# One block for attention and experts in a decoder layer on one core: first shared weights fetched and rounded inside attention, slots computed before other work

## What is computed

```python
x = layernorm(x + state_space_and_mlp(x))           # selective scan, 8 heads, and an MLP of 1024
x = layernorm(x + cross_and_self_attention(x, ctx)) # 16 heads of 128, 4 key/value heads
x = layernorm(x + experts(x))

# experts, on 1024 tokens of 256 channels
scores = sigmoid(x @ w_router.T)                    # 8 experts
topk_w, topk_i = top_k(scores, 2); topk_w /= topk_w.sum(-1)
out = sum over the 2 chosen e: topk_w * ((silu(x @ wg[e].T) * (x @ wu[e].T)) @ wd[e].T)   # inner width 640
out += sum over 2 shared experts j: (silu(x @ sg[j].T) * (x @ su[j].T)) @ sd[j].T
```

## Time and profile before

| what | us |
|---|---|
| median of 3 runs (lowest, highest) | 779.17 (778.35, 784.29) |
| profiled execution | 787.61 |
| its span, first to last instruction | 785.9 |
| PE busy | 722.3 (92%) |
| DVE busy | 564.8 (72%) |
| ACT busy | 472.9 (60%) |
| POOL busy | 344.0 (44%) |

### The profile page before, as it was taken

One profiled execution on the slowest core, in us unless ns is written; L12 is line 12 of the kernel. 1 busy time (PEld: TensorE's weight loads), 2 busy tenths in 40 slices (PEclk: granted clock), 3 DMA queues, 4 the chain that ended last, 5 costly groups with the idle time before them and its releaser, 6 DMA issues. The chain is left out here.

```text
span 785.9 us, 15318 instructions
## 1 busy us (share of the span) xinstructions
PE 722.3 (92%) x5030; PEld 657.3 (84%) x5030; DVE 564.8 (72%) x1176; ACT 472.9 (60%) x1066; POOL 344.0 (44%) x512
## 2 busy tenths in 40 slices
PE   4998888788999999999999987998999999999965
PEld 3887677577889999999899976986999999999855
DVE  4864588876878888887878773664587778776436
ACT  4454666456877777777777772342577777776301
POOL 0002566596988787877787751063000000000341
PEclk9999999998999999999999999699999999999978
DMA  9003300100200000000600000266356766670121
GB/s 290 4 1 115 134 2 0 30 5 28 62 8 1 7 0 7 0 7 0 207 0 0 0 1 9 96 240 209 115 161 227 250 203 210 227 241 28 54 67 54
DMA packets 45940, 64.82 MB, mean 82 GB/s; under 512 B 4288, under 2 KB 34880, under 8 KB 45632
## 3 DMA queue, kind: packets, MB, share of 16 engines
q1 hardware_dynamic: 39936, 56.39, 21.7%
q0 software_dynamic: 1536, 4.20, 1.6%
q10 hardware_dynamic: 4416, 3.58, 1.6%
HBM read 53.14 MB, written 11.01 MB: 82 GB/s over the span
## 5 line engine op out<-in xcount | busy, mean ns | idle before, releaser
L1816 POOL DMA_INDIRECT gu_raw<-rows_out,slot x16 | 15.5, 972 | 203.6 <-DMA rows_out<-y_sb 199.0
L1951 ACT ACTIVATE sg<-bg 128x256 f32<-128x256 f32 (+1 forms) x95 | 40.7, 429 | 104.1 <-PE bg L68 101.6
L413 ACT ACTIVATE under_dt<-two,nb,under_raw 128x256 f32<-128x256 f32 x128 | 70.6, 561 | 45.5 <-DVE nb L496 45.5
L66 PE MATMUL bg<-xb_hi,gu_hi 128*128 128x256 f32 x300 | 87.0, 290 | 2.7 <-DVE xb_lo L2064 2.7
L2041 DVE TENSOR_TENSOR hf<-sg,bg 128x256 f32<-128x256 f32 (+1 forms) x95 | 45.1, 475 | 58.1 <-ACT sg L1951 56.6
L68 PE MATMUL bg<-xb_hi,gu_lo 128*128 128x256 f32 x300 | 85.6, 285 | 0.0
L67 PE MATMUL bg<-xb_lo,gu_hi 128*128 128x256 f32 x300 | 85.5, 285 | 0.0
L66 PE MATMUL two<-under_h 128*128 128x256 f32 (+1 forms) x208 | 66.9, 322 | 2.9 <-PEq L117 1.5
L68 PE MATMUL bd<-dn_hi,eh_lo 128*128 128x256 f32 x220 | 63.1, 287 | 3.9 <-issue 3.8
L67 PE MATMUL bd<-dn_lo,eh_hi 128*128 128x256 f32 x220 | 62.9, 286 | 3.0 <-issue 3.0
L594 POOL TENSOR_SCALAR under_dt<-under_dt,rec 128x256 f32<-128x256 f32 x128 | 61.5, 499 | 6.4 <-DVE rec L542 6.4
(11 more groups left out here) (294 smaller groups left out, 2555.6 us busy)
## 6 DMA issues: line engine op xcount, KB each, us to landing
gu_raw<-in_gu SPq DMA_DIRECT2D x17, 1280.0 KB
dn_raw<-in_dn SPq DMA_DIRECT2D x17, 640.0 KB
rows_in<-under_dt SPq DMA_DIRECT2D x1, 3840.0 KB, 13.1
rows_out<-y_sb SPq DMA_DIRECT2D x30, 128.0 KB, 2.1
x_blk<-rows_in ACTq DMA_DIRECT2D x13, 256.0 KB, 2.7
under_raw<-in_wq SPq DMA_DIRECT2D x1, 2048.0 KB, 8.1
under_raw<-in_wkv SPq DMA_DIRECT2D x1, 2048.0 KB, 12.7
under_raw<-in_wo SPq DMA_DIRECT2D x4, 512.0 KB, 3.9
```

What stands on the lines that cost most here:

```text
L66: pe.matmul(out, lh, rh, start=first, stop=False)
L413: act.activation(self.prob[:, g % 2, h, :], self.b_s[:, h // 2, (h % 2) * MW:(h % 2 + 1) * MW], ACT.Exp, bias=self.nb[:, h:h + 1], scale=s ...
L1816: pool.indirect_dma_start(got[k][:, b, :], None, ys[:, :], bass.IndirectOffsetOnAxis(ap=slot[:, k, b:b + 1], axis=0)).then_inc(f_got[b], 16)
L1951: act.activation(sg[:, u % 3, 0:width(u)], gate_of(u), ACT.Silu).then_inc(f_sg, 1)
```

## The change

Allocation: the experts' buffers are laid out first, over the same memory that attention uses, and released at once, so that both lie over each other; the set of buffers with index 0 and the x buffers are put on the other side. All semaphores of attention and experts are taken in the outermost scope and cleared once at the end. `experts` now returns its engine programs, and each engine's program of attention calls its program of the experts directly, in the same block. What the end of the block ensured is now waited for one by one: PE's transposes wait for the batches they read and for the last readers of the banks that they write; SP and POOL wait for all of `x_tok`.

Order: SP requests the first shared weights after attention's last projection. ACT rounds them in `act_tail`, POOL takes the remainders in `pool_tail` (before: DVE). DVE splits the first quarter of x between the statistics and the rows of batch 7, the last quarter between its first two gates. PE interleaves transposes and logits. `places` comes directly after the gate of unit 1 and before the two splits, `gated(2)` moves up behind it, `rest_dn(0)` and `shares` move to the end of pass 0. All spare products at the seam and in pass 0 go (28, 16 and 28). The load of `upper` moves from ACT's queue to SP's.

The diff, with changes of indentation left out and cut to its core:

```diff
@@ decoder_layer
+        ex = experts(nc, a, scope, sem, ident, x_tok, acc, wr, rank, s_router, xs, ys, s_zero, out)
         with ExitStack() as both:
-            at = Attention(scope(both), nc, a, ident, x_tok, s_zero, xs)
-            state_space_layer(nc, a, scope, ident, x_tok, acc, s_const, at, wr, rank, s_router)
-        experts(nc, a, scope, ident, x_tok, acc, wr, rank, s_router, xs, ys, s_zero, out)
+            at = Attention(scope(both)[0:2] + (sem,), nc, a, ident, x_tok, s_zero, xs, ex)
+            state_space_layer(nc, a, scope, sem, ident, x_tok, acc, s_const, at, wr, rank, s_router)
@@ act_tail
         self.act_p(act, N1)
+        self.ex.act_weights(act, 0)
+        self.ex.act_weights(act, 1)
         self.act_exp(act, 3, N3)
@@ dve_tails
         self.dve_tail(dve, LAST)
+        self.ex.dve_x(dve, 0)
         self.dve_tail2(dve, LAST)
@@ pool_tail
             self.pool_step(pool, LAST, g, False, True)
+            if g >= 2:
+                self.ex.pool_weights(pool, g - 2)
@@ Attention.sp_program
+        sp.wait_ge(self.a_pj, NS)
+        self.ex.load_first(sp)
@@ Attention.pe_program
         self.over_batches(pe, self.pe_step, self.pe_tail)
-        self.pe_spare(pe, self.b_q[:, 0:DM], 28)
@@ state_space_layer (and the same for sp, pool, act, dve)
                     aw.pe_program(pe)
+                    aw.ex.pe_program(pe, aw)
@@ experts
+        def load_first(sp):
+            sp.dma_start(gu_raw[0][:, :, :, :], a["gu"][E].rearrange("s (k p) n -> p s k n", p=P)).then_inc(e_gu[0], 16)
+            sp.dma_start(dn_raw[0][:, :, :], a["dn"][E].rearrange("(i p) n -> p i n", p=P)).then_inc(e_dn[0], 16)
+        def act_weights(act, s):
+            if s == 0:
+                act.wait_ge(e_gu[0], 16)
+            act.activation(gu_hi[0][:, s, :, :], gu_raw[0][:, s, :, :], ACT.Copy).then_inc(w_gh[0], 1)
+        def pool_weights(pool, s):
+            pool.wait_ge(w_gh[0], s + 1)
+            pool.tensor_tensor(gu_lo[0][:, s, :, :], gu_raw[0][:, s, :, :], gu_hi[0][:, s, :, :].bitcast(F32),
+                               ALU.subtract).then_inc(w_gl[0], 1)
+        def dve_x(dve, q):
+            s = slice(q * 256, (q + 1) * 256)
+            dve.wait_ge(r_f, q + 1)
+            dve.tensor_copy(x_hi[:, :, s], x_f[:, :, s]).then_inc(r_hi, 1)
+            dve.wait_ge(r_hi, q + 1)
+            dve.tensor_tensor(x_lo[:, :, s], x_f[:, :, s], x_hi[:, :, s].bitcast(F32), ALU.subtract).then_inc(r_lo, 1)
@@ experts, sp
-                load(0)
+            sp.wait_ge(at.a_x2, BATCH)
+            sp.wait_ge(s_zero, 16)
+            sp.dma_start(upper[:, :], a["upper"]).then_inc(r_c2, 16)
             load(1)
@@ experts, pool
+            pool.wait_ge(at.a_x2, BATCH)
+            pool.wait_ge(s_zero, 16)
@@ experts, pe
-                for q in range(4):
+            def turn_x(q):
+                pe.wait_ge(at.a_x2, 2 * q + 2)
+                if q == 0:
+                    pe.wait_ge(at.a_exp, NS * AREP)
+                elif q == 2:
+                    pe.wait_ge(at.a_olo, NS)
...
-                pe.wait_ge(r_lo, 1)
-                spare(pe, bx[1][:, 0:256], x_hi[:, 0, 0:P], x_hi[:, 0, 0:256], 16)
+            turn_x(0)
+            turn_x(1)
+            turn_x(2)
+            pe.wait_ge(s_router, 32)
+            for b in range(4):
+                logits(b)
+            turn_x(3)
+            for b in range(4, BATCH):
+                logits(b)
             for q in range(NG_):
...
-                    if q == 0:
-                        spare(pe, bd[1][:, 0:256], x_hi[:, 0, 0:P], x_hi[:, 0, 0:256], 28)
@@ experts, act
-                act.dma_start(upper[:, :], a["upper"]).then_inc(r_c2, 16)
...
-                round_gu(0, 0)
-                round_gu(0, 1)
@@ experts, dve
-                rest_gu(0, 0)
-                rest_gu(0, 1)
+            dve_x(dve, 1)
+            dve_x(dve, 2)
             dve.wait_ge(r_l, 1)
+            dve.wait_ge(s_zero, 16)
...
+                if q == 0:
+                    dve_x(dve, 3)
                 gated(IT * q + 1)
+                if q == 0:
+                    places()
+                    gated(2)
                 rest_h(IT * q)
...
                 if q == 0:
-                        places()
                     owners()
-                        rest_dn(0)
-                        shares()
...
+                if q:
                     gated(IT * q + 2)
...
                 rest_h(IT * q + 3)
+                if q == 0:
+                    rest_dn(0)
+                    shares()
```

More of the change, by code:

```diff
@@ L7 @@
+from collections import namedtuple
 from contextlib import ExitStack
@@ L158, with __init__ @@
 class Attention:
-    def __init__(self, ctx, nc, a, eye, x_tok, s_zero, xs):
+    def __init__(self, ctx, nc, a, eye, x_tok, s_zero, xs, ex):
         self.sb, self.ps, self.sem = ctx
-        self.nc, self.a, self.eye, self.x_tok, self.s_zero, self.xs = nc, a, eye, x_tok, s_zero, xs
+        self.nc, self.a, self.eye, self.x_tok, self.s_zero, self.xs, self.ex = nc, a, eye, x_tok, s_zero, xs, ex
         self.turn = {}
@@ L731, in pool_program, with state_space_layer @@
         pool.tensor_tensor(r1[:, :], ve[:, :], mh[:, 0:1], ALU.pow).then_inc(self.a_r1, 1)
-def state_space_layer(nc, a, scope, ident, x_tok, acc, s_const, aw, wr, rank, s_router):
+def state_space_layer(nc, a, scope, kept, ident, x_tok, acc, s_const, aw, wr, rank, s_router):
     with ExitStack() as layer:
-        sb, ps, sem = scope(layer)
         h_hi, h_lo, win_hi, win_lo = aw.h_hi, aw.h_lo, aw.win_hi, aw.win_lo
@@ L1146, in state_space_layer @@
         with ExitStack() as part:
-            sb, ps, sem = scope(part)
+            sem = kept
             TW = 2 * P
@@ L1221, in _ @@
                     aw.sp_program(sp)
+                    aw.ex.sp_program(sp, aw)
                 @block.gpsimd
@@ L1645, in outputs_before, with experts @@
     return sum(4 if shared(g) else 2 for g in range(q))
-def experts(nc, a, scope, ident, x_tok, accm, wr, rank, s_router, xs, ys, s_zero, out):
+Programs = namedtuple("Programs", ("load_first", "act_weights", "pool_weights", "dve_x", "sp_program", "pool_program",
+                                   "pe_program", "act_program", "dve_program"))
+def experts(nc, a, scope, sem, ident, x_tok, accm, wr, rank, s_router, xs, ys, s_zero, out):
     NG_ = NBLK + 4
@@ L1651, in experts @@
     ROOTS = ((0, 4), (4, 6), (6, 8))
[L1652 to L1660, removed]
+    with ExitStack() as over:
+        sb, ps, _ = scope(over)
+        side = lambda i: "right" if i == 0 else None
+        gu_raw = [sb(f"gu_raw{i}", [P, 2, KT, FI], F32, side(i)) for i in range(2)]
+        dn_raw = [sb(f"dn_raw{i}", [P, IT, DM], F32, side(i)) for i in range(2)]
+        gu_hi = [sb(f"gu_hi{i}", [P, 2, KT, FI], F32R, side(i)) for i in range(2)]
+        gu_lo = [sb(f"gu_lo{i}", [P, 2, KT, FI], F32R, side(i)) for i in range(2)]
+        x_hi = sb("x_hi", [P, KT, TOK], F32R, "right")
+        x_lo = sb("x_lo", [P, KT, TOK], F32R, "right")
+        x_f = sb("x_f", [P, KT, TOK], F32, "right")
         dn_hi = [sb(f"dn_hi{i}", [P, IT, DM], F32R) for i in range(2)]
```

897 lines of the change are left out of this document (444 added, 453 removed).

## The result

| | median of runs, us (lowest to highest) | profiled, us | span, us |
|---|---|---|---|
| before, the 3 runs known at first | 779.17 (778.35 to 784.29) | 787.61 | 785.9 |
| before, with the 6 taken beside the change | 783.28 (778.35 to 786.56) | | |
| the change, 9 runs | 772.57 (770.26 to 779.31) | 770.26 | 768.6 |

The ratio is 0.9874, 95% interval 0.9846 to 0.9902: some 9.9 us faster (7.7 to 12.1). The forecast was 765.7 with a saving of 13.5; 772.57 lies above its range. The sign was right, the time was not.

What follows compares the result with a forecast made beforehand. PE's spare products, waits and half clock at the seam between attention and experts were taken as the loss. A gain of 16.5 us less 3.0 for the clock, 13.5 off 779.17, gave 765.7 us; range 761.5 to 770.

Steps and rivals of the forecast that it cites:

- POOL's remainders, taken at nothing: Attention's tail: POOL takes the first shared weights' remainders, 3.0 us each, inside its idle time, at no cost.
- the base of 779.17: Median of the runs shown, 8.4 us under the profiled one; the forecast took its saving off this.
- Transposes and router: Seam: transposes directly follow attention's last product, router records take 0.12 us each, PE through at 489.4 instead of 498.07.
- Weights on ACT: Attention's tail: ACT rounds the first shared weights, 2.43 us, inside a 2.65 us wait, at no cost.
- A stretched tail: Sign that the prediction is wrong: attention's tail itself stretches, with exponentials after 469.
- First quarter of x: End of attention: DVE makes it while waiting for POOL's root; last x_tok slips by 0.1 us, at no cost.
- Places, fifth unit: First shared pass: slots at 500.0, 14.6 us earlier; the fifth unit starts at 500.8 instead of 518.22.
- Scatter late next by 0.9: First routed block: its rows arrive at 528.5, PE at 527.6, so PE waits 0.9 us; gain there 16.5 us.
- The clock: Seam: PE's clock falls during transposes and 8-column router records, costing 3.0 us, bounds 0 and 4.1.
- clock stays up: Rival, chance 0.24: the clock does not fall at the seam, saving 16.5 us, time 762.7.
- The seam as a whole: From attention's end to the first routed block: 16.5 us gained less 3.0 for the clock, 13.5 us off.
- The rival of a slower time: Chance 0.03: the clock does not come back, both shared passes run at half clock, time 793 us.

Runs made afterwards that it cites:

- e7: e1 with DVE's rounding of the first quarter of x moved behind the last normalised tokens; 769.47 us, ratio 0.9824 to the kernel before.
- e1: The change with both POOL remainders of the first shared weights moved behind its last attention step; on three chips 772.83, 768.42, 772.16 us (ratios 0.9871, 0.9797, 0.9850).
- e2: The change with two groups of 8 spare PE products added among the seam's transposes and router products; 773.08 us, ratio 0.9846 to the kernel before.
- e6: The change with each POOL subtraction of 128x1280 cut into ten of 128x128 in the same place; 770.93 us, ratio 0.9826 to the kernel before.
- e3: The change with DVE's order in pass 0 put back as in the kernel before; 779.14 us, ratio 0.9943 to the kernel before.

## Why the prediction failed, step by step

Two terms put the measured 772.57 above the range: POOL's remainders, taken at nothing, cost attention's tail 1.7 us, and the base of 779.17 was 4.1 us low. With the later base the forecast would have been 769.8, with the tail's 1.7 us as well 771.5.

- **Transposes and router: right.** They follow attention's last product directly. The record that no row had priced takes 1.92 / 16 = 0.12 us at full clock, the value taken. The 0.60 us of ACT's copy was read from a silu of the same shape; the copies took 0.60 too.
- **Weights on ACT: right**, inside its idle time. **Remainders on POOL, "nothing": wrong.** The step looked at idle time on POOL's own queue and not at what DVE does meanwhile. It cost 1.7 us in attention's tail. A stretched tail was named as what would refute the forecast, but by the time 469 of the profile before: this execution reached the tail 2.7 us sooner (PE's wait of 1.23 us for the same tile stands at 462.61, before at 465.28), so its 468.00 hides the delay, and only the durations and waits show it. **First quarter of x, 0.1 us: small error**, 0.5 of the same kind (e7).
- **Places, fifth unit: right.** With the clock up `x_tok` to slots is 13.2 us (e1); the forecast has 500.0 - 485.8 = 14.2 to their end, 14.0 to the start that the table counts. The fifth unit waits for nothing, and from it to the turn PE works 26.9 us (forecast 26.8).
- **Scatter late next by 0.9: not so.** At 529.67 PE does not wait for the rows. SP issues their load at 525.58, 23.7 us after the end of the slots, where the prediction kept the old 25.6.
- **The clock: size right, cause incomplete.** Its fall cost 3.1 us at the slots (forecast 3.0, of 0 to 4.1). But transposes and 8-column records alone do not let it fall: e1 has 5.6 us of nothing else (481.74 to 487.34) at 1.00. By the Trainium skill, page "TensorE: Matmul & The Clock Gate", Part 4 (PE-mode transpose), the full clock does not engage in transposes; here a clock that was up stayed up through twelve of them in a row with the router's records behind. Idle time ahead of them is the likelier cause (3.12 us in the change, 1.42 in e1), but e2 and e6 leave it open. The rival "clock stays up" (16.5 us) has the clock of e1; its saving, 15.9 and 11.8 us beside the change and 10.1 alone by e1's ratios, is that large, within its interval, only in the first of the three.
- **The seam as a whole: right.** From `x_tok` to the turn the profiles before give 59.2 and 57.6 us (mean 58.4), the change 44.3, 44.4 and 46.6 (45.1): 13.3 us off, forecast 13.5. Less the 1.7 us of the tail, 11.6 are left; three comparisons measured 9.9, 12.4 and 8.5. The remaining us lies within their intervals and isn't settled.
- **The base: wrong.** 4.1 us of the miss of 6.9 are the median of three runs, 779.17, that the nine put at 783.28; 2.8 are saving (10.7 between the medians). The profiled 787.61, 8.4 above, should have widened the range upwards: the kernel's own runs go from 778.35 to 790.88.

Range: it held the unknown prices of the seam, and neither the base nor a meeting of two engines. The rival of a slower time didn't occur; the clock was back by 496. After the turn nothing was lost: from it to the end of the span are 240.9 and 241.2 us before, 238.9, 238.1 and 241.0 in the change.

## What to carry to other kernels

Work moved into an engine's idle time isn't free before one has looked at what the other engine of the pair DVE and POOL does in that time: a long POOL instruction can hold a tiny DVE one with two SBUF operands until its end, and if that stands on the critical chain, cutting the long one or moving it a few us mends it. Look for the idle time ahead of a fall of the clock, not only at the kind of work under it. And take the scatter of the runs into the range, above all when the profiled execution stands far from a median of three.

## What the runs showed of the hardware that was not expected

- A DVE operation of 0.16 us took 1.84 or 1.86 us beside one POOL subtraction of 2.95 or 2.96 us, in all five profiles in which they met (three of the change, e2, e3), and 0.20 beside ten short ones. Ten pieces cost POOL 4.26 us against 2.96.
- The same meeting works the other way: POOL's root on 128x1 took 1.01 us beside DVE's `x_lo` of two SBUF operands and 0.56 without it.
- One kernel's stretch of low clock at one place can differ twofold between executions, with 3.3 us at the slots of the kernel before.
- With DMA at some 400 GB/s PE stood up to 1.76 us (e6) between two down products with nothing in the profile that it waited for; the cause is open.
